# A two-layer pair kernel: the second norm's statistics by batch-norm statistics per chunk, its roots in three steps, the gates in other banks

## The reference

```python
# layer one
xn = layernorm(x) * ln1_w + ln1_b
left  = sigmoid(xn @ left1)  * (xn @ left2)
right = sigmoid(xn @ right1) * (xn @ right2)
p = einsum('nsre,nkre->nske', left, right)      # 32 products of 128 x 128
p = layernorm(p) * ln2_w + ln2_b                # the second norm, over the 32 features e
x1 = x + (p @ out_w) * sigmoid(xn @ gate)
# layer two
l = x1 @ W_left + b_left + x1 @ W_eq + b_eq
rs = sum of (x1 @ W_right + b_right) over one token axis
o = l * rs * sigmoid(x1 @ W_gate + b_gate)
out = layernorm(o @ W_out + b_out + x1) * ln_scale + ln_bias
```

## Time and profile before

| | |
|---|---|
| median of 3 runs | 117.25 us (116.78 to 118.27) |
| the profiled execution | 117.17 us, span 115.4 us |
| PE busy | 91.1 us (79% of the span), 566 matmuls |
| DVE busy | 81.5 us (71%) |
| ACT busy | 69.5 us (60%) |
| POOL busy | 69.6 us (60%) |
| mean granted PE clock | 0.909 |
| HBM read, written | 2.31 MB, 2.10 MB |

### The profile page before, as it was taken

One profiled execution on the slowest core, in us unless ns is written; L12 is line 12 of the kernel. 1 busy time (PEld: TensorE's weight loads), 2 busy tenths in 40 slices (PEclk: granted clock), 3 DMA queues, 4 the chain that ended last, 5 costly groups with the idle time before them and its releaser, 6 DMA issues.

```text
span 115.4 us, 1799 instructions
## 1 busy us (share of the span) xinstructions
PE 91.1 (79%) x566; PEld 70.7 (61%) x566; DVE 81.5 (71%) x239; ACT 69.5 (60%) x121; POOL 69.6 (60%) x83
## 2 busy tenths in 40 slices
PE   1929796099999899996929999999999999795000
PEld 1925484067677699752415587989888797794000
DVE  1538459976978907769997372857798897999910
ACT  0521967578787369981469837476995997841100
POOL 5048923799990008845703988587834869994800
PEclk9995579959999999999995999999999999999755
DMA  3589994000000000000000000000000005539796
GB/s 61 111 135 168 145 145 40 0 0 6 0 0 0 3 6 3 0 0 0 0 0 0 0 6 0 0 3 0 0 0 6 0 10 80 91 47 143 109 145 101
DMA packets 33484, 4.51 MB, mean 39 GB/s; under 512 B 33348, under 2 KB 33476, under 8 KB 33476
## 3 DMA queue, kind: packets, MB, share of 16 engines
q1 hardware_dynamic: 31632, 4.00, 26.6%
q10 hardware_dynamic: 1844, 0.41, 1.8%
HBM read 2.31 MB, written 2.10 MB: 38 GB/s over the span
## 4 chain that ended last, share of the span: by engine, by line
PE 51%; DVE 18%; POOL 8%; issue 6%; ACT 5%; DMA 5%; SPq 1%; DVEq 0%; POOLq 0%
PE bank L820 12%; PE bank L910 6%; PE bank L953 6%; POOL acc_q L356 6%; DMA x_tok<-in_x 5%; PE bank L962 5%; PE bank L805 4%; PE bank L924 3%; PE bank L927 3%; PE bank L925 3%; PE bank L883 3%; DVE lr L741 3%; DVE lr L590 3%; PE bank L899 2%; POOL xc L285 2%
## 5 line engine op out<-in xcount | busy, mean ns | idle before, releaser
L820 PE MATMUL bank<-lr_blk,xnT 64*128 64x256 f32 x128 | 19.2, 442 | 3.3 <-ACT xnT L431 3.1
L590 DVE TENSOR_TENSOR lr<-bank,sig_lr 128x512 f32<-128x512 f32 x16 | 15.8, 1044 | 4.7 <-ACT sig_lr L441 4.6
L372 POOL TENSOR_TENSOR x_low<-x1T,x_high 128x512 fp32r<-128x512 f32 x8 | 11.0, 1378 | 12.1 <-ACT x_high L497 12.1
L820 PEld LDWEIGHTS bank<-lr_blk,xnT 64*128 64x128 f32 x128 | 13.3, 211 | 6.9 <-POOL lr_blk L303 2.5
L364 POOL TENSOR_TENSOR t_tok<-p_sb,rstd 128x512 f32<-128x512 f32 x7 | 10.4, 1492 | 2.8 <-DVE rstd L698 2.8
L441 ACT ACTIVATE sig_lr<-bank 128x512 f32<-128x512 f32 x16 | 9.6, 597 | 3.9 <-PE bank L820 3.8
L388 POOL TENSOR_TENSOR sq<-lr,row_rep 128x512 f32<-128x512 f32 x7 | 9.8, 1398 | 2.0 <-DVE lr L744 2.0
L285 POOL TENSOR_TENSOR xc<-x_tok,stats 128x512 f32<-128x512 f32 (+1 forms) x8 | 8.1, 1010 | 4.7 <-DVE stats L575 4.7
L575 DVE BATCH_NORM_STATS2 stats<-x_tok 128x6 f32<-128x64 f32 x64 | 8.8, 211 | 2.8 <-DMA x_tok<-in_x 2.8
L910 PE MATMUL bank<-tT,out_blk 128*128 128x512 f32 x16 | 8.9, 643 | 2.2 <-DVE x1T L715 2.2
L380 POOL TENSOR_TENSOR oT<-o_a,rsum 128x512 f32<-128x512 f32 x8 | 8.7, 1087 | 2.5 <-issue 1.9
(11 more groups left out here) (114 smaller groups left out, 215.5 us busy)
## 6 DMA issues: line engine op xcount, KB each, us to landing
x_tok<-in_x SPq DMA_DIRECT2D x14, 128.0 KB, 4.2
out<-sq SPq DMA_DIRECT2D x7, 256.0 KB, 3.3
x_tok<-in_x SPq DMA_DIRECT2D x3, 64.0 KB, 2.5
w_rep<-in_weights ACTq DMA_DIRECT2D x1, 180.5 KB
out<-sq ACTq DMA_DIRECT2D x1, 128.0 KB, 4.6
out<-sq SPq DMA_DIRECT2D x1, 128.0 KB, 4.9
x_tok<-in_x ACTq DMA_DIRECT2D x1, 64.0 KB, 2.7
row_rep<-in_rows ACTq DMA_DIRECT2D x1, 32.0 KB, 5.1
```

The source lines that it names most:

```text
L372: nc.gpsimd.tensor_tensor(x1_low[:, c % 2], x1T[:, c % 3], x1_high[:, c % 2], ALU.subtract).then_inc(x1_low_ready, 1)
L590: nc.vector.tensor_tensor(lr[:, :, s].rearrange("p f s -> p s f"), src[:, :, 2 * CH:4 * CH], sig_lr[:, j % 3].rearrange("p (s f) -> p s f" ...
L820: last = nc.tensor.matmul(dst, xnT[half, c, k * P:(k + 1) * P], lr_blk[half].rearrange("p g m c -> p g (m c)"), start=True, stop=True, ski ...
```

## The change

- ACT no longer squares the banks. `p_sq`, `acc_p`, `acc_q`, POOL's five adds and DVE's adds and `variance2` go.
- In their place DVE runs `statistics2(c)`: 8 batch-norm statistics instructions for a chunk, each over one pair of tokens (64 values a partition), read from `p_sb`. They need all eight banks. The third statistic of each token goes to the root with a scale of 1/32.
- `ROOTS2` gives three roots: chunks 0 and 1, chunks 2 and 3, chunks 4 to 7. The first is taken before the loop, the second in step 1, the third at the end of ACT's step 2.
- The gates of chunks 0 to 4 go to banks 3 to 7, those of 5 to 7 to banks 6, 7 and 6 again. `gate0(0)` to `gate0(3)` are taken one or two at a time, `gate0(4)` to `gate0(7)` at the end of step 2.
- POOL's `normalise2` stands in another place: steps 0 and 1 make chunk `i+2` as before, step 2 none, steps 3 to 6 chunk `i+1`.

```diff
-POOL_SQ = 6
-FIRST2 = 3 * SPC
-GATE0_BANK = [0, 1, 3, 4, 5, 6, 7, 3]
-GATES_FIRST = 2
+ROOTS2 = [(0, 2), (2, 4), (4, 8)]
+GATE0_BANK = [3, 4, 5, 6, 7, 6, 7, 6]
@@ POOL
-            for b in range(1, POOL_SQ):
...
-                nc.gpsimd.tensor_tensor(acc_q[:, 0], prev, p_sq[:, 4 * b:4 * b + 4, :],
-                                        ALU.add).then_inc(pool_step if b < POOL_SQ - 1 else squares_pool, 1)
             def normalise2(c):
-                pool.wait_ge(rstd2, 1 if c * SPC < FIRST2 else 2)
+                pool.wait_ge(rstd2, holding(ROOTS2, c) + 1)
...
-                if i + 2 < CHUNKS:
+                if i < 2:
                     normalise2(i + 2)
+                elif 3 <= i < CHUNKS - 1:
+                    normalise2(i + 1)
@@ ACT
-                nc.scalar.activation(p_sq[:, 4 * b:4 * b + 4, :], src, ACT.Square).then_inc(psq_ready, 1)
...
+            def root2_of(b):
+                first, last = ROOTS2[b]
+                act.wait_ge(stats2_ready, last)
+                root(1, first * SPC, last * SPC, root2)
+            root2_of(0)
+            gate0(0)
             for i in range(CHUNKS + 3):
                 if i < CHUNKS:
                     evacuate_tT(i)
+                if i == 0:
+                    gate0(1)
                 if i == 1:
-                    act.wait_ge(var2, 2)
-                    root(1, FIRST2, P, root2)
-                    for c in range(GATES_FIRST, 5):
-                        gate0(c)
+                    root2_of(1)
                 if i == 2:
-                    for c in range(5, CHUNKS):
-                        gate0(c)
+                    gate0(2)
+                    gate0(3)
                     act.wait_ge(biases, 3)
...
                     gate1(i - 2)
+                if i == 2:
+                    for c in range(4, CHUNKS):
+                        gate0(c)
+                    root2_of(2)
@@ DVE
+            def statistics2(c):
+                if c == 0:
+                    dve.wait_ge(p_ready, 8)
+                for k in range(c * SPC, (c + 1) * SPC, 2):
+                    last = nc.vector.bn_stats(stats2[:, k:k + 2, :].rearrange("p s v -> p (s v)"), p_sb[:, :, k:k + 2])
+                last.then_inc(stats2_ready, 1)
+            def inverse2(b):
+                s = slice(ROOTS2[b][0] * SPC, ROOTS2[b][1] * SPC)
+                dve.wait_ge(root2, b + 1)
+                nc.vector.reciprocal(rstd[:, 1, s], std[:, 1, s]).then_inc(rstd2, 1)
+            statistics2(0)
+            statistics2(1)
+            inverse2(0)
...
+            statistics2(2)
+            statistics2(3)
...
                 if i == 1:
+                    inverse2(1)
+                    statistics2(4)
+                    statistics2(5)
+                if i == 2:
+                    statistics2(6)
+                if i == 3:
+                    inverse2(2)
...
+                if i == 2:
+                    statistics2(7)
@@ PE
-            for c in range(6):
+            for c in range(4):
                 project_gate0(c)
-                if c == 3:
-                    transpose_x(0)
+            transpose_x(0)
...
                 if i == 0:
-                    project_gate0(6)
+                    project_gate0(4)
...
-                if i == 2:
-                    project_gate0(7)
...
                     project_1(i - 2)
+                if i == 2:
+                    for c in range(5, CHUNKS):
+                        project_gate0(c)
```

More of the change, by code:

```diff
@@ L419, in root @@
                     values, of = stat(std[:, 0], lo, hi), place(stats1[:, :, 2:3], lo, hi)
+                elif layer == 1:
+                    of = stats2[:, lo:hi, 2]
                 nc.scalar.activation(values, of, ACT.Sqrt, scale=1.0 / CH, bias=eps[:]).then_inc(done, 1)
@@ L480, in gate0 @@
                 nc.scalar.activation(gT[:, c], bank[:, GATE0_BANK[c]], ACT.Sigmoid).then_inc(g_ready, 1)
-            for c in range(GATES_FIRST):
-                gate0(c)
-            act.wait_ge(var2, 1)
-            root(1, 0, FIRST2, root2)
+            def root2_of(b):
[4 more added lines that the diff above has]
+            gate0(0)
             def evacuate_tT(c):
@@ L646, in _ @@
             nc.vector.tensor_scalar(right_bias[:], right_bias[:], float(P), None, ALU.mult).then_inc(biases, 1)
-            def tick(instruction):
-                steps[0] += 1
-                instruction.then_inc(step, 1)
-                return steps[0]
-            for b in range(1, 7):
-                dve.wait_ge(psq_ready, b + 1)
-                if b > 1:
-                    dve.wait_ge(p_added, b - 1)
-                prev = p_sb[:, 0:4, :] if b == 1 else acc_p[:]
-                nc.vector.tensor_tensor(acc_p[:], bank[:, b].rearrange("p (e s) -> p e s", e=4), prev, ALU.add
-                                        ).then_inc(p_added, 1)
@@ L690, in _ @@
-            first, rest = slice(0, FIRST2), slice(FIRST2, P)
-            dve.wait_ge(psq_ready, 8)
-            dve.wait_ge(p_added, 6)
-            add_last_p(first)
-            dve.wait_ge(squares_pool, 1)
-            variance2(first, 7)
-            add_last_p(rest)
-            dve.wait_ge(root2, 1)
-            nc.vector.reciprocal(rstd[:, 1, first], std[:, 1, first]).then_inc(rstd2, 1)
+            def statistics2(c):
[4 more added lines that the diff above has]
+                last.then_inc(stats2_ready, 1)
@@ L759, in _ @@
                 if i == 1:
-                    dve.wait_ge(root2, 2)
-                    nc.vector.reciprocal(rstd[:, 1, rest], std[:, 1, rest]).then_inc(rstd2, 1)
+                    inverse2(1)
[5 more added lines that the diff above has]
+                    inverse2(2)
                 if i <= CHUNKS:
@@ L868, in project_gate0 @@
                 b = GATE0_BANK[c]
-                pe.wait_ge(psq_ready, b + 1)
-                if b:
-                    pe.wait_ge(p_added, b if b < 7 else 8)
+                pe.wait_ge(p_ready, b + 1)
                 if b in GATE0_BANK[:c]:
-                    pe.wait_ge(g_ready, GATE0_BANK.index(b) + 1)
+                    pe.wait_ge(g_ready, max(n for n in range(c) if GATE0_BANK[n] == b) + 1)
                 nc.tensor.matmul(bank[:, b], gate0_blk[:], xnT[:, c], start=True, stop=True).then_inc(g_ps, 1)
@@ L879, in transpose_x @@
                 else:
-                    pe.wait_ge(p_added, XT)
+                    pe.wait_ge(p_ready, XT + 1)
                 for j in range(BLK):
```

44 lines of the change are left out of this document (6 added, 38 removed).

## The result

| | before | after |
|---|---|---|
| median of the comparison | 117.76 us (116.78 to 118.85) | 133.94 us (132.47 to 135.5) |
| ratio, 95% interval | | 1.1354 [1.1277, 1.1431] |
| a second comparison, another chip | 116.79 us | 132.94 us (132.46 to 134.53), ratio 1.1379 [1.1307, 1.1451] |
| the profiled execution shown below | 117.17 us, span 115.4 | 132.6 us, span 130.8 |
| PE, DVE, ACT, POOL busy | 91.1, 81.5, 69.5, 69.6 us | 95.3, 78.8, 73.0, 63.4 us |

The changed kernel is 13.5% slower.

A forecast was written before the change was run, and what follows sets the result against it. PE's pace was taken to bound the third stage. Loop 10.9 and passage 0.4 give 11.3 us, with 3.0 for the clock 14.3, on 117.17: 131.5 us, range 127.5 to 136.

The forecast's parts named there:

- the likeliest case: Whole kernel: loop and clock cost what the sum gives, 131.5 us; chance 0.58.
- The loop's chain: Third stage, chunks 3 to 7: PE waits each step for POOL's t_tok, together 10.9 us more.
- The waits: PE stands 3.9 us ahead of chunk 2, 4.1 (chunk 4), 1.9 (5), 2.8 (6) and 1.9 (7).
- The table load: Step 3, ahead of gate1(1) on ACT: the diff's load puts 1.30 us on the chain from chunk 3 to 4.
- The rival with a drain: Three table loads on or near the chain each some 1.4 us dearer: 135.5 us; chance 0.03.
- The passage: Between the stages, up to chunk 3: a 1.9 us earlier start is given back to the second root, 0.4 us lost.
- The clock: PE at half clock after three long waits, 3.3 us each, 1.0 us on the chain for each: 3.0 us.
- its rival of 135 us: Half clock lasts 6.7 us instead of 3.3, or waits of 1.9 us bring it too: 135 us; chance 0.12.
- Its first half: Passage up to chunk 0: sixteen statistics take 2.11 us, PE gets chunk 0 at about 52.3 instead of 54.22.
- The last step: Third stage, chunk 6 to 7: an even step, 1.93 us longer by the wait for POOL's t_tok.

The follow-up runs named there:

- The kernel with the order alone: The kernel before with only POOL's new place for normalise2 (chunk i+1 in steps 3 to 6), second norm untouched: 129.25 us, ratio 1.0907.
- the kernel kept busy: The changed kernel with identity products on PE ahead of the transposes of chunks 2, 4 and 6: 131.2 us, ratio 1.1062.
- the kernel with three chunks first: The changed kernel with roots split at chunks 3 and 5, POOL's old order, gates 0 and 1 ahead of the first root: 117.76 us, ratio 1.0062.
- the fastest kernel: New statistics, roots split at chunks 3 and 5, POOL's old order and the gates' banks of before, against the kernel before: 115.43 us, ratio 0.9846.
- the first experiment: The changed kernel with POOL's order put back, so normalise2 makes chunk i+2 in step i again: 123.35 us, ratio 1.0503.

## Why the prediction was right

The forecast was 131.5 us in a range from 127.5 to 136, slower with 0.93. Measured: 133.94, and 132.94 in the second comparison. The direction, the mechanism and the range held; the likeliest case came, with a forecast 1.4 to 2.4 us too low. 0.6 of the 2.4 are in the base, 117.76 us for the kernel before in that comparison where the sum started from 117.17. Point by point:

- **The loop's chain** was right. Summed for full clock: 4.18 for chunk 3 to 4, measured 4.31; 1.93 for 4 to 5, at full clock 2.09; 2.87 for 5 to 6, measured 2.93; 1.93 for 6 to 7, measured 2.39. The kernel with the order alone reproduced three of the four distances to 0.05 us.
- **The waits** forecast ahead of chunks 2, 4 and 6 were 3.9, 4.1 and 2.8 us; they are 3.81, 3.92 and 2.71. Ahead of chunk 5 it was 0.67 in place of 1.9, because PE worked through that step at half clock and came late itself; with the clock kept up it was 1.85.
- **The table load** on the chain, 1.30, measured 1.43. The rival with a drain fell: after the load that ends at 73.14 the sigmoid began at 73.16. The Trainium skill, "ScalarE: Activation LUTs", section "What ACT_TABLE_LOAD costs", gives about 2.66 us for a switch with its drain; the rows show no drain, and the measurement decides. The Trainium skill's advice on the same page, section "Table sets: the hidden batching unit", to batch activations by set is borne out in kind: the load that was taken off the chain had cost 1.43 us there. What the other loads cost was not measured one by one.
- **The passage** was too small a term. The sum had +0.4; at full clock it is +0.69, and the half clock beside chunk 2's wait makes it +2.06. Most of the 0.29 at full clock lie ahead of gate 6: it began 16.77 us after the last product in the kernel kept busy, where the sum had 16.5. Two gates up to chunk 3 took 1.79 us, as summed (1.76).
- **The clock.** The sum had 3.0 us, for three stretches of 3.3 us at 1.0 us on the chain each. That waits of this length bring half clock and that it reaches the chain was right. In the shown profile it came twice, beside the waits for chunks 2 and 4: 1.37 us in the passage and 1.34 in step 4 to 5, 2.7 in all. The second lasted 6.8 us, about the length that the prediction had given to its rival of 135 us. In the 135.5 us execution there was a third, worth 1.46 us. So number, length and price were each off, and that 2.7 lies so near to 3.0 is luck.
- **Its first half** was right to 0.2 us: 16 statistics in 2.12 us (forecast 2.1, 2.11), so the pitch of 512 bytes costs nothing; chunk 0 on PE 4.66 us after the last product, where the forecast had 4.7. The early start was given back as forecast, to the second root.

```profile
48.46 2.12 DVE L651 BATCH_NORM_STATS2 stats<-p_sb 128x6 f32<-128x64 f32 x16 [7.57 <-ACT p_sb L466]
```

- **The last step**, 0.46 above its forecast, was not foreseen. Its `low1` lasts longer:

```profile
97.74 0.69 DVE L708 TENSOR_TENSOR lr<-lr,row_rep 128x512 f32<-128x512 f32 x1
97.84 1.71 POOL L359 TENSOR_TENSOR x_low<-x1T,x_high 128x512 fp32r<-128x512 f32 x1 [4.31 <-ACT x_high L490]
```

It takes 1.71 us where the earlier trace rows have 1.29, beside a DVE instruction with two inputs in SBUF; before, the same pair stood at 89.77 (1.74 us), with the chunk long made, and the kernel with the order alone has it at 93.29 (1.75 us). A term that was hidden came onto the chain when the chunk was put behind it. Adding up all that was missed: 0.13 (3 to 4) + 0.16 (4 to 5) + 0.06 (5 to 6) + 0.46 (6 to 7) + 0.29 (passage) + 0.28 (ahead of the stretch and behind it) is 1.38, less 0.29 for the clock 1.09: the difference between the 14.3 us of the sum and the 15.4 us between the two spans.

What stays open is which of the waits of some 2.7 us brings half clock: seven are seen in these profiles, five of them with it and two without. Nor was it tried what the last step costs without the `low1` that meets DVE's multiply.

## What to carry to other kernels

Where engines work through hand-ordered lists, a helper's result costs its place within the step more than the number of steps it is made ahead: put what the main engine asks for next ahead of anything that hangs on that engine's present step. The price of such a move can be read beforehand, from the distance in the old trace between the main engine's start of a step and the end of the helper's instruction at the new place, less the step's own length. Split a chain of roots or statistics where the consumer first needs them, and count a table load at its full length where an activation behind it is waited for, as in the one place tried here.

## What the runs showed of the hardware

- Each of the seven waits of PE of 3.8 or 3.9 us in the third stage went with half clock (granted clock 0.50). It cost 0.4 us on the chain where it began 1.2 us after PE went on, 1.1 where it began 0.5 us after, and 1.3 to 1.4 where it began before. After waits of 2.70 to 2.72 us it came five times (at 88.17 in the kernel with the order alone, for one) and stayed away twice (at 73.22 in the same profile, and at 93.58 after the change).
- Shorter waits do not settle it. Half clock followed after 1.91 us (the kernel with three chunks first), 2.05 us (the fastest kernel), 2.17 us and 2.29 us (PE kept busy); none followed after 1.97 us (POOL's order put back) and twice after 2.18 us (the order alone at 59.80, the changed kernel at 100.90). Forecasts should count it with a chance there.
- With identity products in PE's waits the clock stayed at 1.00 from 56 to 99 us. The kernel that waits was some 3 points faster with them (1.1062 against 1.1379).
- The products between stages one and three took 7.41 us in nine profiles and 9.04 in two, at half clock, for the same instructions with the same wait of 0.54 us ahead of them (39.78 in the first experiment). A difference of 1.5 us between two single runs can come from this alone.
- POOL's `low1` took 1.71 us beside a DVE multiply that reads two tiles from SBUF and had begun 0.10 us sooner, and 1.27 us at 72.00 without one. The Trainium skill, "SBUF — State Buffer", section "Who interferes with whom", says that a DVE instruction with two SBUF inputs and a GpSimd one that reads SBUF contend, and that issue order decides which of them blocks. The rows agree: the later one, on POOL, was 0.44 us longer.
